# Query bias on TensorE, parts cast from the bank, zeros multiplied at the start, residual additions moved

## The reference

```
# layer 0                                   # layer 1
q = layernorm(x) @ Wq + bq                  d = layernorm(x);  q = d @ Wq.T + bq
attn = softmax(q k^T / sqrt(8))             attn = softmax(q k^T)
x = x + (attn v) @ Wo + bo                  x = x + norm(attn v + d) * gamma + beta
```

## Time and profile before

| What | Value |
|---|---|
| median of three executions | 343.8 us (342.59 to 346.49) |
| profiled execution, own time | 343.55 us |
| its span, first to last instruction | 341.8 us |
| TensorE matmul / weight load busy | 313.5 us (92%) / 158.6 us (46%) |
| VectorE, ScalarE, GpSimd busy | 270.7 (79%), 213.3 (62%), 71.2 us (21%) |
| chain that ended last, by engine | PE 66%, DVE 17%, ACT 8%, issue 6% |

### The profile page before, as it was taken

One profiled execution on the slowest core, in us unless ns is written; L12 is line 12 of the kernel. 1 busy time (PEld: TensorE's weight loads), 2 busy tenths in 40 slices (PEclk: granted clock), 3 DMA queues, 4 the chain that ended last, 5 costly groups with the idle time before them and its releaser, 6 DMA issues.

```text
span 341.8 us, 6071 instructions
## 1 busy us (share of the span) xinstructions
PE 313.5 (92%) x2284; PEld 158.6 (46%) x2284; DVE 270.7 (79%) x690; ACT 213.3 (62%) x260; POOL 71.2 (21%) x131
## 2 busy tenths in 40 slices
PE   5889999999999999888998999989999999999970
PEld 2545545877785562554522234342322344645530
DVE  3898857723687868899999999999998834588996
ACT  3649797674867874547755777977998995003000
POOL 4263520100200374303370241011001200011000
PEclk9999999999999999999999999999999999999995
DMA  6930000000000000000000000000000000000001
GB/s 228 417 128 2 3 2 1 0 2 1 2 0 2 0 3 0 2 2 1 2 0 1 2 0 2 0 2 0 2 0 2 2 2 0 2 0 0 1 0 61
DMA packets 2044, 7.48 MB, mean 22 GB/s; under 512 B 224, under 2 KB 608, under 8 KB 1632
## 3 DMA queue, kind: packets, MB, share of 16 engines
q1 hardware_dynamic: 2016, 7.11, 5.5%
HBM read 6.58 MB, written 0.52 MB: 21 GB/s over the span
## 4 chain that ended last, share of the span: by engine, by line
PE 66%; DVE 17%; ACT 8%; issue 6%; POOL 1%; DMA 1%; POOLq 0%; SPq 0%; ACTq 0%; DVEq 0%
PE ring_ps L609 39%; PE out_ps L609 12%; PE misc_ps L609 7%; DVE mx L1204 6%; ACT pT L988 4%; PE misc_ps L770 1%; PE ring_ps L732 1%; PE misc_ps L826 1%; DVE ACC L1380 1%; DVE Z L1053 1%; DVE ACC L1053 1%; PE misc_ps L645 1%; ACT XN L915 1%; PE ring_ps L826 1%; PE ring_ps L645 1%
## 5 line engine op out<-in xcount | busy, mean ns | idle before, releaser
L988 ACT ACTIVATE pT<-ring_ps 128x1024 f32<-128x1024 f32 (+1 forms) x96 | 94.2, 1026 | 25.0 <-PE ring_ps L609 24.0
L1204 DVE TENSOR_REDUCE mx<-ring_ps 128x2 f32<-128x1024 f32 (+1 forms) x96 | 98.8, 1075 | 7.8 <-PE ring_ps L609 7.3
L609 PE MATMUL ring_ps<-XT,f 128*128 128x512 f32 x96 | 44.3, 601 | 0.0
L538 POOL TENSOR_TENSOR rstd<-var,consts 128x4 f32<-128x4 f32 (+1 forms) x15 | 14.7, 978 | 136.4 <-DVE var L1071 73.9
L609 PE MATMUL out_ps<-pT,V 128*32 128x512 f32 x256 | 34.9, 605 | 0.0
L577 POOL TENSOR_SCALAR pT<-pT 77x1024 f32<-77x1024 f32 x8 | 22.7, 2845 | 46.3 <-ACT pT L988 46.3
L609 PE MATMUL ring_ps<-f,hid 128*128 128x512 f32 (+1 forms) x96 | 31.9, 486 | 0.0
L1380 DVE SCALAR_TENSOR_TENSOR X<-ring_ps,gw,X 128x128 f32<-128x128 f32 x64 | 18.0, 344 | 16.8 <-PE ring_ps L609 16.5
L609 PEld LDWEIGHTS ring_ps<-f0y,hid 128*128 128x128 f32 x256 | 29.6, 192 | 2.4 <-issue 1.9
L609 PE MATMUL ring_ps<-f0y,hid 128*128 128x128 f32 x256 | 30.4, 276 | 0.0
L609 PE MATMUL misc_ps<-identb 128*128 128x512 bf16 x78 | 23.7, 396 | 4.1 <-DVE identb L1473 4.1
(11 more groups left out here) (187 smaller groups left out, 461.5 us busy)
## 6 DMA issues: line engine op xcount, KB each, us to landing
f<-in_f SPq DMA_DIRECT2D x1, 1669.0 KB, 14.1
f<-in_f SPq DMA_DIRECT2D x1, 1028.0 KB, 7.5
f0y<-in_f0y SPq DMA_DIRECT2D x1, 1024.0 KB, 9.5
X<-in_x SPq DMA_DIRECT2D x2, 256.0 KB, 4.0
wb<-in_wb SPq DMA_DIRECT2D x1, 512.0 KB, 10.3
rows<-in_rows SPq DMA_DIRECT2D x1, 512.0 KB, 10.8
trig<-in_trig SPq DMA_DIRECT2D x1, 512.0 KB, 10.9
wa<-in_wa SPq DMA_DIRECT2D x1, 333.0 KB, 4.1
```

What stands on the lines that cost most here:

```text
L538: return pool.tensor_tensor(out, a, c, op)
L609: return nc.tensor.matmul(out, lhsT, rhs, start=start, stop=stop)
L988: nc.scalar.activation(probs_buf(layer, i, kt)[0:parts_, 2 * half:2 * half + 2, :], ring_ps[ring.buf(step)][0:parts_, :, :], ACT.Exp, scal ...
L1204: V_.tensor_reduce(dst, src, AX.X, ALU.max).then_inc(ring.read_sem(step), 1)
```

## The change

The query bias of layers 0 and 1 is multiplied on TensorE: a row of ones (1 partition, 128 weights) with the bias row repeated four times (512 columns, fp32) opens the bank, and the four products of the projection are added to it. The bias product stands behind the identity matmuls and ahead of the wait for XT. TensorE waits for the rows and for the ones. VectorE's step `QP` casts the first part from the bank and subtracts it from the bank; `SPLITQ` does the two remaining operations. For the second and third part nothing changes, nor in layer 2. The counters of the parts are divided in two (`PART0`, `PART1`); that code and the removal of an unused split on GpSimd are cut below.

TensorE multiplies zeros nine times (512 columns, bf16) before it waits for the constants; VectorE clears the zeros first of all, GpSimd sets the ones first of all. `CKV 0` has two identity matmuls ahead of it instead of four. The residual additions stand behind `MCH` of the last group of each half (layer 0), and behind the guard of the second group of each half (layer 1).

```diff
@@ -50,6 +50,7 @@
+WARM_UP = 9
 SLOTS = 6
...
@@ -71,7 +71,7 @@
              ("ST", 1, 4, 0, 0): 3, ("KT", 0, 0): 10, ("ST", 1, 5, 0, 0): 3, ("MTR", 2, 1): 4,
-             ("ST", 2, 1, 0, 0): 3, ("KT", 1, 0): 3, ("OTR", 2, 3): 1, ("CKV", 0): 4, ("XT", "n0", 0, 0): 1,
+             ("ST", 2, 1, 0, 0): 3, ("KT", 1, 0): 3, ("OTR", 2, 3): 1, ("CKV", 0): 2, ("XT", "n0", 0, 0): 1,
              ("XT", "n0", 0, 1): 1, ("XT", "n0", 0, 2): 1, ("XT", "n0", 0, 3): 1, ("MTR", 0, 0): 1}
...
@@ -281,6 +281,8 @@
         rows0 = sb("rows0", [P, ROWS0 * P])
+        zeros = sb("zeros", [P, P], BF16)
+        ones = sb("ones", [1, P])
         rows = sb("rows", [P, (len(ROWS) - ROWS0) * P])
...
@@ -503,6 +505,7 @@
         def _(pool):
+            pool.memset(ones[:, :], 1.0).then_inc(ones_set, 1)
             for b in range(B):
...
@@ -545,10 +548,8 @@
-            def NORM(step, kind, b):
-
-                if kind not in ("n0", "n2"):
-                    return
+            def shift_rows(kind, b):
+
                 pool.wait_ge(loaded["rows0" if kind == "n0" else "rows"], 16)
...
@@ -567,6 +568,8 @@
                 tt(c[:, :, :, 2], r, c[:, :, :, 1], ALU.subtract).then_inc(done["MCHP"], 1)
+                if layer == 0 and i % GR == GR - 1:
+                    shift_rows("n0", i // GR)
...
@@ -575,29 +578,10 @@
                 pool.tensor_scalar(heads, heads, 0.0, None, ALU.max).then_inc(done["GUARD"], 1)
-
-            def SPLITQ(step, layer, b):
...
-
-            parts = {"STAT": STAT, "NORM": NORM, "FIN1": FIN1, "MCH": MCH, "ST": ST, "SPLITQ": SPLITQ, "ENDS": ENDS}
+                if i % GR == 1:
+                    shift_rows("n2", i // GR)
+
+            parts = {"STAT": STAT, "FIN1": FIN1, "MCH": MCH, "ST": ST, "ENDS": ENDS}
             for step in schedule:
...
@@ -645,13 +629,16 @@
                 last.then_inc(misc.full_sem(step), 1)
-            def project(step, b, w, width, xt_step):
+            def project(step, b, w, width, xt_step, bias=None):
                 wait_free(misc, step)
                 keep_busy(step, small_ps(step))
+                if bias is not None:
+                    mm(small_ps(step), ones[:, :], bias[0:1, :].unsqueeze(1).broadcast_to([1, T, width]), stop=False)
                 pe.wait_ge(*misc.read(xt_step))
                 for t in range(T):
-                    last = mm(small_ps(step)[:, t * width:(t + 1) * width], XT[b][:, t * P:(t + 1) * P], w)
+                    last = mm(small_ps(step)[:, t * width:(t + 1) * width], XT[b][:, t * P:(t + 1) * P], w,
+                              start=bias is None, stop=bias is None or t == T - 1)
                 last.then_inc(misc.full_sem(step), 1)
...
@@ -659,7 +646,10 @@
                 else:
                     pe.wait_ge(loaded["wa"], 16)
-                project(step, b, wq[layer], P, ("XT", ("n0", "n2", "n4")[layer], b))
+                if layer < 2:
+                    pe.wait_ge(ones_set, 1)
+                    pe.wait_ge(loaded["rows" if layer else "rows0"], 16)
+                project(step, b, wq[layer], P, ("XT", ("n0", "n2", "n4")[layer], b), row[f"bq{layer}"] if layer < 2 else None)
             def OP(step, layer, b):
...
@@ -892,6 +882,9 @@
                      "FH": FH, "FY": FY, "GH": GH, "SO": SO, "RO": RO}
+            pe.wait_ge(zeros_set, 1)
+            for _ in range(WARM_UP):
+                mm(misc_ps[:, :], zeros[:, :], zeros[:, :].unsqueeze(1).broadcast_to([P, 4, P]))
             pe.wait_ge(loaded["consts"], 16)
...
@@ -1112,10 +1105,11 @@
                     return slot(cat, first, pairs, s, parts)
                 s0, s1, s2 = (part_of.index(k) for k in range(3))
-                V_.tensor_copy(dst(s0), flat_heads(values)).then_inc(done["PART"], 1)
-                dve.wait_ge(*after("PART", *step, 0))
-                link(tt(flat_heads(rest), flat_heads(values), dst(s0), ALU.subtract))
-                V_.tensor_copy(dst(s1), flat_heads(rest)).then_inc(done["PART"], 1)
+                if values is not None:
+                    V_.tensor_copy(dst(s0), flat_heads(values)).then_inc(done["PART0"], 1)
+                    dve.wait_ge(*after("PART", *step, 0))
+                    link(tt(flat_heads(rest), flat_heads(values), dst(s0), ALU.subtract))
+                V_.tensor_copy(dst(s1), flat_heads(rest)).then_inc(done["PART1"], 1)
                 dve.wait_ge(*after("PART", *step, 1))
                 return tt(dst(s2), flat_heads(rest), dst(s1), ALU.subtract)
...
@@ -1138,8 +1132,10 @@
                 src = small_ps(step).rearrange("p (t d) -> p t d", t=T)
                 if layer < 2:
-                    tt(QF[b].rearrange("p (t d) -> p t d", t=T), src, over_tiles(row[f"bq{layer}"]),
-                       ALU.add).then_inc(misc.read_sem(step), 1)
+                    part = slot(qcat[b], 0, T * H, Q_PART.index(0))
+                    V_.tensor_copy(part, flat_heads(small_ps(step))).then_inc(done["PART0"], 1)
+                    dve.wait_ge(*after("PART", "SPLITQ", layer, b, 0))
+                    tt(flat_heads(RS[b]), flat_heads(small_ps(step)), part, ALU.subtract).then_inc(misc.read_sem(step), 1)
                     dve.wait_ge(*misc.read(step))
                 else:
...
@@ -1148,13 +1144,13 @@
             def SPLITQ(step, layer, b):
-                if (layer, b) in POOL_SPLITS:
-                    return
                 if layer == 0:
                     dve.wait_ge(zeroed, 1)
                 if layer == 2:
                     dve.wait_ge(*after("QROT", b))
-                split(step, qcat[b], 0, T * H, QF[b], RS[b], Q_PART).then_inc(done["SPLITQ"], 1)
+                else:
+                    dve.wait_ge(*misc.read(("QP", layer, b)))
+                split(step, qcat[b], 0, T * H, QF[b] if layer == 2 else None, RS[b], Q_PART).then_inc(done["SPLITQ"], 1)
             def KV(step, b):
...
@@ -1467,6 +1463,7 @@
                      "OUT": OUT, "ENDS": ENDS, "ENDN": ENDN}
+            V_.memset(zeros[:, :], 0.0).then_inc(zeros_set, 1)
             link(V_.memset(columns(kcat, 0, T * H, MROW, HS - MROW), 0.0))
...
```

More of the change, by code:

```diff
@@ L370, in build @@
         kinds = {"NORM": "normed", "NORMR": "scaled",
-                 "SPLITQ": "query_parts", "SPLITQ_POOL": "pool_query_parts", "SPLITC": "context_parts", "SPLITK": "key_parts",
+                 "SPLITQ": "query_parts", "SPLITC": "context_parts", "SPLITK": "key_parts",
                  "MCH": "max_parts", "MCHP": "pool_max_parts", "FH": "hidden", "RT": "router_diffs", "RTE": "router_exps",
@@ L374, in build @@
                  "FIN1": "cross_attended", "PV": "pv", "NORMSTATS": "stats", "RSTD": "rstds",
-                 "OUTV": "out_rows", "GUARD": "guarded", "GUARDV": "dve_guarded", "OC": "out_ps_read", "OTRX": "attended_rows", "PART": "parts", "PARTP": "pool_parts",
+                 "OUTV": "out_rows", "GUARD": "guarded", "GUARDV": "dve_guarded", "OC": "out_ps_read", "OTRX": "attended_rows", "PART0": "first_parts", "PART1": "second_parts",
                  "DUPQ": "query_copies", "DUPK": "key_copies", "DUPC": "context_copies", "QP": "rotated_queries"}
@@ L398, in after @@
             if kind == "PART":
-                on_pool = args[:1] == ("SPLITQ",) and args[1:3] in POOL_SPLITS
-                same = [s for s in splits if (s[0] == "SPLITQ" and s[1:] in POOL_SPLITS) == on_pool]
-                return done["PARTP" if on_pool else "PART"], 2 * same.index(args[:-1]) + args[-1] + 1
+                split_, k = args[:-1], args[-1]
+                if k == 0 and split_[:1] == ("SPLITQ",) and split_[1] < 2:
+                    split_ = ("QP",) + split_[1:]
+                return done[f"PART{k}"], part_steps[k].index(split_) + 1
             if kind == "QROT":
                 return done["QP"], [s for s in schedule if s[:2] == ("QP", 2)].index(("QP", 2) + args) + 1
-            if kind in ("SPLITQ", "SPLITQ_POOL"):
-                same = [s for s in schedule if s[0] == "SPLITQ" and (s[1:] in POOL_SPLITS) == (kind == "SPLITQ_POOL")]
-                return done[kind], same.index(("SPLITQ",) + args) + 1
             return done[kind], nth[(base.get(kind, kind),) + args]
@@ L417, in build @@
         hidden = [s[1:] for s in schedule if s[0] == "FH"]
-        splits = [s for s in schedule if s[0] in ("SPLITQ", "SPLITK", "SPLITC")]
+        part_steps = ([s for s in schedule if s[0] in ("SPLITK", "SPLITC") or s[:2] == ("SPLITQ", 2) or
+                       s[0] == "QP" and s[1] < 2],
+                      [s for s in schedule if s[0] in ("SPLITQ", "SPLITK", "SPLITC")])
         maxes = [s[1:3] for s in schedule if s[0] == "SMAX" and s[3:] == (0, 0)]
@@ L443, in build @@
         stored = [sem(f"stored{b}") for b in range(B)]
-        zeroed = sem("zeroed")
+        zeroed, ones_set = sem("zeroed"), sem("ones_set")
         last_bank0 = sem("last_unit_bank0_full")
@@ L449, in build @@
         consts_cast = sem("consts_cast")
+        zeros_set = sem("zeros_set")
         dve_chain = sem("dve_chain")
@@ L577, in ST @@
```

(25 more changed lines are left out.)

3 lines of the change are left out of this document (removed).

## The result

The changed kernel took 347.97 us (median of 4 runs, 347.14 to 349.36) beside 344.84 us of the kernel before (4 runs, 342.59 to 346.49). It is slower by 3.1 us, or 0.9% by these two medians; the ratio on record is 1.0116, interval 1.0074 to 1.0158. The time is above the range of the forecast. The profiled execution took 347.14 us (span 345.4) against 343.55 (span 341.8): +3.6 us. The profiled execution of the kernel before is not one of its shortest: in three later series, 79 executions, 23 have a span of 340.7 to 341.2, none a lower one. From lowest to lowest (342.50 to 347.14) the change costs 4.6 us. What the shorter executions do otherwise no trace shows.

The account below looks back on a forecast made before the run. VectorE decides from 160 to 180 us, TensorE's own queue from 27.24 and 97.60 us. Second query, third, fourth and guard: 0.74 + 0.86 - 0.42 + 0.52 = +1.7 on 343.55 gives 345.2 us; range 342.5 to 347.0.

Parts of the forecast that it names:

- So 0.86 us each, four in all: Each query's one-row bias product on TensorE costs 0.86 us, sized from 512-column fp32 expert products; bounds 0 and 0.86.
- The ones load as weights under earlier work: At the bias products, TensorE's load of the ones was to be hidden under earlier work, at no cost.
- Start: First query: earlier XT copy and shorter VectorE work, less the bias, make its transposes start 0.73 us earlier.
- Second query: Bias and VectorE's two operations ahead of the maxima copy delay it 1.47 us, +0.74 after the start's 0.73.
- Third query: TensorE's own queue is the chain there, so the bias product costs its full +0.86 us.
- Fourth query: Up to VectorE's gamma multiplication: bias 0.83, less 0.43, 0.04 and 0.78, makes -0.42 us.
- The credit of 0.78 for the moved addition: Fourth query: moving GpSimd's residual addition away lets VectorE's cast take 0.43 instead of 1.21 us.
- loses +0.52: VectorE's guard at 171.68 us is held until GpSimd's moved addition ends at 172.2; bounds 0 and 0.8.
- the fallen level: TensorE's clock level falls in a longer wait before the scores at 24 us: 2.4 us, total 347.7; chance 0.07.
- the hidden bias: TensorE waits hide the bias product behind the second to fourth query: -0.85, total 342.7 us; chance 0.25.
- the cold start: Zeros do not raise TensorE's level earlier, so the start is 0.19 late: +2.6, total 346.2 us; chance 0.13.
- Three of the additions cost the chain nothing: Two first-layer additions and that of the second layer's first half fall into GpSimd's idle time: 0; without it 1.3 each.

Follow-up runs that it names:

- experiment 5: Changed kernel with the bias product over 128 rows (ones in row 0 of the weights, zeros below) instead of one row: 345.97 us.
- experiment 2: Changed kernel with the two residual additions of layer 1 back at their old places: 345.86 us.
- experiments 10: Changed kernel with the bias added on VectorE at all four queries, keeping the zeros and the four moved additions: 344.68 us.
- experiment 11: Changed kernel with bias on VectorE at all queries and layer 1's additions at the old place (first half) and about 147 us (second half): 342.82 us.
- Experiments 2 and 7: The second of these: experiment 6 with layer 1's additions at the old place (first half) and about 147 us (second half): 343.21 us.
- experiment 9: The changed kernel measured again, nothing altered, in the session of the other experiments: 348.92 us.
- experiment 6: Changed kernel with bias product and bank cast only at the first and fourth query, bias on VectorE at the second and third: 344.17 us.
- experiment 1: Changed kernel with the bias product left out at all four queries: 342.92 us.
- experiment 3: Kernel before with only the nine products of zeros and two identity matmuls ahead of the context projection: 342.47 us.
- experiment 12: Experiment 8 with the bias product over 128 rows and two identity matmuls kept ahead of the fourth query's transposes: 341.08 us.
- experiment 8: Experiment 6 with layer 1's additions off the guards and one-row products replacing identity matmuls at the first query and ahead of the fourth's transposes: 342.24 us.

## Why the prediction was wrong

At the places that the forecast named the bias, the cast and the held guard did what it said, but several costs were too small, and two collisions behind the guard were not in it. Against the profiled execution it said +1.7 us and +3.6 was measured. The terms:

- **"So 0.86 us each, four in all" is the first step that failed.** The nearest rows were products with a contraction of 128, whose successors load their weights ahead. The one-row product lets nothing load ahead: 1.05 us to the next product at each of the four (experiment 5 gives 0.86 with 128 rows, 0.94 at the second query). "The ones load as weights under earlier work" failed too: at the third query they load at 97.69, with the product, after 0.76 us of an idle loader. I named the missing price (no product with a contraction of 1 in the trace) and then bounded it above by the nearest row; the bound should have been open upward.
- **Start: -0.34 instead of -0.73.** XT copy (8.9 forecast, 8.86 measured) and cast from the bank (0.69, both) were right. 0.19 is the product, 0.09 its later start, 0.11 a gap ahead of the second cast. The Trainium skill, VectorE: DVE Perf Modes, "Why PSUM operands drop a tier", gives an fp32 operand in PSUM the slowest mode; the trace agrees, with 0.69 for the cast from the bank and 0.43 for that from SBUF.
- **Second query: +1.67 on its own instead of +1.47**, the product's 0.19. The order in VectorE's queue, cast and subtraction ahead of the maxima, was right.
- **Third query: +1.26 instead of +0.86.** 1.05 for the product; the product itself starts 0.95 us after the last expert load, where the projection of before took 0.86; and from projection to experts 1.44 us pass instead of 1.33.
- **Fourth query: -0.20 instead of -0.42**, again the product. The credit of 0.78 for the moved addition was booked to the wrong part, as experiment 2 shows: this cast would have passed the addition at its old place too. Nor is it worth its full size at the end of the kernel (experiments 10 and 11).
- **Guards: "loses +0.52" is the second step that failed, +1.3 measured.** The held guard is there, 0.32 long. The 0.52 took the guard to start over when the addition ends; the forecast's own row says less, for the cast at 138.66 lost 0.78 to an addition that overlapped it by 0.92. Here the overlap is 0.44 and the loss 0.32. What I did not follow is what comes next: that delay moves the product with `rinv` into GpSimd's next guard (+0.75) and the second guard too (+0.27). Experiments 2 and 7 give 1.4 and 1.3 back. I stopped at the first collision, though the earlier trace rows had the GpSimd guard at 172.94, and the product with `rinv` started 0.19 us ahead of it in the kernel before (172.75): a delay of 0.32 had to push it in. The Trainium skill, SBUF — State Buffer, "Who interferes with whom", states that GpSimd and such a VectorE operation exclude each other for the whole instruction, the one that starts first holding the other. The guard agrees: it ends at 175.04, behind the addition's end at 174.49. The product with `rinv` does not: it was held 0.75 us beside a GpSimd guard that ran to about 178, so here the measurement decides: not each pair waits to the end. In the kernel before, a VectorE guard that started at 121.08 within a GpSimd guard (119.37 to 122.66) took its usual 0.69, and it was the GpSimd guard that took 3.29 instead of 2.76. Which of two is held, and for how long, these traces do not settle.

Start, second and third query, fourth and guards miss by 0.39 + 0.20 + 0.40 + 0.22 + 0.80 = 2.0 us; 0.1 comes back near the end. That is 347.1. The experiments agree: the 128-row product takes back 1.3 us, and the guards' excess is 0.8.

The rest, up to the median of 347.97, is **the fallen level**, which had 0.07 of the chance. It came near the place that was named, but not for the reason given. The rival had it fall in TensorE's longer wait at 24 us; in experiment 9 it fell at about 21.3 us, during the bias product and ahead of that wait, and in experiment 6 it fell at about 20.7 us without any longer wait. That the rival's 347.7 lies near the median is in part luck. By their times it fell in six of eight executions, by a trace in one of two. Its cost was about right in size: 1.1 to 2.2 us here, 2.4 forecast. The chance was too low because I reasoned from one profiled execution of the kernel before, in which it did not fall, and did not ask how often it does in others.

Of the rivals, the hidden bias is excluded (experiment 1: the four products cost 4.3 us together), and so is the cold start (with the zeros the level is up by 7 us, experiment 3). Three of the additions cost the chain nothing, as forecast. The one of the second layer's first half (124.68 to 126.38, 1.70 long instead of 1.26) does collide: with it the VectorE guard at 123.97 takes 1.28 (0.69 in experiment 2, without it), and an operation at 128.37 takes 0.77 instead of 0.17. But VectorE's next copy of `oT` stands at 127.63 with it and at 127.61 in experiment 2, and the product with `rinv` ahead of the fourth query at 134.90 and 134.89.

**Open** is why the level falls. It fell in the one-row kernels (6 of 8 executions of the change, 3 of 10 in experiment 2), in 1 of 10 with the product over 128 rows and in none of 8 in experiment 12, but by the same reading also in 5 of 10 of experiment 11 and 2 of 10 of experiment 3, which have no bias product at all, and in 4 of 10 of experiment 6, where the trace has it fall in a query without one. A product with few rows is thus not needed for it. These are counts of long times, most of them without a trace. That the level falls more often in the changed kernel than in the kernel before is not shown either: of the kernel before only one execution has a trace, and its times spread more.

## What to carry to other kernels

Price an instruction of a shape that the trace does not show by what the next one can do beside it, not only by its own columns: here the one-row product costs 1.05 instead of 0.86, and 128 rows with zeros are the cheaper way to add a row. Take more than one trace of the kernel before, if its times spread by more than the change is worth. Follow a delay on the limiting engine past the first instruction that it hits; here the second collision cost more than the first. A gain for one engine (0.43 us of VectorE per query) is worth nothing where another engine's queue is the chain; keep an addition to TensorE to the places where it waits. There it can stand in for some of the fillers; in experiment 8 it stood in for seven, all that stood at its two places, and the level fell in the profiled execution.

## What the runs showed of the hardware

- While a matmul with a contraction of one row runs (512 columns, fp32) the weight loader is idle 0.76 us, and the next product starts 1.05 us after it; over 128 rows the next weights load 0.43 us ahead and it is 0.86 (experiment 5).
- Nine products of zeros, from 0.97 us, raise TensorE's level: it is high at 7.03 us, when without them it rose at about 8.95.
- The level fell to 1.2 GHz while TensorE was busy (1.00 of the microsecond from 21 us, granted 0.66), some 2 us after a stretch in which it was busy half of the time (0.50 and 0.46 from 17 to 19 us), and came back after some 7 us. After the same stretch it stayed up in another execution of the same kernel.
- Executions with a fallen level can decide the median at this scale: the kernel of experiment 12, whose trace shows no fall before the end, had eight runs within 0.2 us, the other changed kernels 0.8 to 2.8 us of spread.
